# Local attention: the floor under the sums of squares as a maximum over pairs, its power of two moved into the logarithm and the Newton step

## The reference, cut to what matters

```python
def l2norm(t):
    return t / jnp.clip(jnp.linalg.norm(t, axis=-1, keepdims=True), 1e-12)

def _layer(x, wqkv, qs, ksc, wo, lg, lb, w1, b1, w2, b2):
    h = shift_token(x)
    q, k, v = jnp.split(h @ wqkv, 3, axis=-1)
    q, k, v = (to_heads(q), to_heads(k), to_heads(v))
    q = l2norm(q) * qs
    k = l2norm(k) * ksc
    q, k = rotary_xpos(q, k)
    o = local_attention(q, k, v)
    ...
```

## Time and profile before

| | |
|---|---|
| median of 3 runs (lowest, highest) | 3533.75 us (3529.92, 3533.93) |
| the profiled execution | 3536.04 us, span 3534.4 us, mean granted clock 0.947 |
| PE busy | 3087.3 us, 87% |
| DVE busy | 2690.6 us, 76% |
| ACT busy | 1625.1 us, 46% |
| POOL busy | 839.8 us, 24% |
| L2017 | 128 times, 168.5 us, mean 1316 ns |
| L2025 idle before it, waiting for L1827 | 54.9 us, 40 times |
| local attention, first layer | L2014 from 2057.97 to 2568.16 us |
| local attention, second layer | L2014 from 2775.85 to 3307.19 us |

### The profile page before, as it was taken

The page is one execution under the profiler, slowest core; times in us unless marked ns, Lnnn a source line. Parts: engine busy times, 40 slices in busy tenths (PEclk is TensorE's granted clock), DMA queues, the critical chain, the costliest instruction groups (busy, mean ns, idle before and its releaser), DMA issues. The chain is left out here.

```text
span 3534.4 us, 95348 instructions
## 1 busy us (share of the span) xinstructions
PE 3087.3 (87%) x34384; PEld 2089.7 (59%) x34384; DVE 2690.6 (76%) x5841; ACT 1625.1 (46%) x2545; POOL 839.8 (24%) x892
## 2 busy tenths in 40 slices
PE   4998769998999979999899668898979788888787
PEld 2666656665666656666566446666655456656545
DVE  5887767886777767766688779999956689989655
ACT  2665115664333335543466435555532355555422
POOL 1000000000000000001000156666611466666311
PEclk9999559998999989999899879999999999999999
DMA  4110001110000021110111100000001000000022
GB/s 137 30 29 20 0 5 31 29 29 4 0 0 0 0 44 38 41 22 1 28 27 29 62 13 7 9 9 8 4 19 27 13 11 10 9 11 8 19 65 59
DMA packets 193061, 80.16 MB, mean 23 GB/s; under 512 B 179124, under 2 KB 181864, under 8 KB 192232
## 3 DMA queue, kind: packets, MB, share of 16 engines
q1 hardware_dynamic: 191592, 73.25, 8.9%
q0 software_dynamic: 1280, 4.20, 0.3%
HBM read 35.58 MB, written 8.39 MB: 12 GB/s over the span
## 5 line engine op out<-in xcount | busy, mean ns | idle before, releaser
L770 ACT ACTIVATE probs_t<-ps_pt 128x1024 f32<-128x1024 f32 x256 | 262.2, 1024 | 384.8 <-PE ps_pt L884 384.8
L632 DVE TENSOR_REDUCE row_max<-ps_s 128x16 f32<-128x1024 f32 x256 | 313.2, 1224 | 135.2 <-PE ps_s L873 132.5
L1961 POOL TENSOR_TENSOR kblk<-kblk 128x1024 f32<-128x1024 f32 x128 | 301.6, 2356 | 199.1 <-DVE kblk L2002 199.1
L637 DVE TENSOR_TENSOR probs<-ps_s,row_max 128x1024 f32<-128x1024 f32 x256 | 312.1, 1219 | 11.7
L906 PE MATMUL ps_o<-v,probs_t 128*64 128x18 f32 x8192 | 285.4, 212 | 5.4 <-issue 5.2
L616 POOL TENSOR_TENSOR x<-x,out_bias_L 128x512 f32 (+1 forms) x32 | 40.7, 1272 | 1030.3 <-DVE x_norm L426 520.8
L906 PEld LDWEIGHTS ps_o<-v,probs_t 128*64 128x64 f32 x8192 | 260.1, 138 | 40.3 <-issue 19.0
L884 PE MATMUL ps_pt<-ident,probs 128*128 128x128 f32 x2048 | 277.1, 278 | 2.9 <-ACT probs L765 2.9
L873 PE MATMUL ps_s<-kblk,q_t 64*64 64x512 f32 x2048 | 273.5, 607 | 7.0 <-issue 6.9
L765 ACT ACTIVATE probs<-probs 128x1024 f32<-128x1024 f32 x256 | 269.6, 1053 | 16.6 <-DVE probs L637 15.1
L1979 POOL TENSOR_TENSOR kblk<-kblk,small_d 128x1024 f32<-128x1024 f32 x128 | 243.6, 1903 | 50.7 <-POOL small_d L1971 50.7
(11 more groups left out here) (307 smaller groups left out, 6930.7 us busy)
## 6 DMA issues: line engine op xcount, KB each, us to landing
ci<-in_ctx_t SPq DMA_DIRECT2D x64, 256.0 KB, 3.0
kblk<-k_t SPq DMA_DIRECT2D x768, 16.0 KB
ci<-x SPq DMA_DIRECT2D x64, 128.0 KB
ci<-x SPq DMA_DIRECT2D x128, 63.0 KB
x<-in_x_in SPq DMA_DIRECT2D x4, 1024.0 KB, 8.0
mask<-in_mask_l SPq DMA_DIRECT2D x64, 64.0 KB, 2.5
kblk<-ci SPq DMA_DIRECT2D x256, 16.0 KB
out<-x SPq DMA_DIRECT2D x1, 4096.0 KB, 11.1
```

Of the source, the lines that this page charges most:

```text
L632: dve.tensor_reduce(row_max[u % 2][:, :], scores_of(u), AX, ALU.max).then_inc(max_ready.sem, 1)
L637: dve.tensor_tensor(probs[u % 2][:, :, :], scores_of(u), row_max[u % 2][:, :].unsqueeze(2).broadcast_to([P, HEADS, S]), ALU.subtract).then ...
L770: act.activation(probs_t[:, :, :], ps_pt[:, :, :].rearrange("p a (r t) -> p (a r) t", t=P), ACT.Copy).then_inc(pt_ready.sem, 1)
L1961: pool.tensor_tensor(a, a, b_, ALU.add).then_inc(rotated.sem, 1)
```

## The change

The sums of squares are written to every second element of a new buffer `floored` (128 x 16 x 2), whose other elements hold the floor 1e-24, filled once in `prepare_layers`. A maximum over pairs (a reduction) replaces the two-operation instruction that took the maximum and multiplied by 2^20. The power of two goes into the scale of the logarithm's input and into the factor of the Newton step.

```diff
+        floored = sb("floored", [P, 2 * LHEADS, 2])
...
                 @block.vector
                 def _(dve):
+                    dve.memset(floored[:, :, 1], 1e-24).then_inc(tables.sem, 1)
...
-            nwork, nrm, nlog, nroot, nstep = (small[n][:, 0, :] for n in "abcde")
+            nrm, nlog, nroot, nstep = (small[n][:, 0, :] for n in "bcde")
...
-                        act.activation(nlog, nrm, ACT.Ln).then_inc(l_root.sem, 1)
+                        act.activation(nlog, nrm, ACT.Ln, scale=float(2 ** LOG_SCALE)).then_inc(l_root.sem, 1)
...
-                        step(pool.tensor_scalar(nstep, nstep, -0.5, 1.5, ALU.mult, ALU.add))
+                        step(pool.tensor_scalar(nstep, nstep, -0.5 * 2 ** LOG_SCALE, 1.5, ALU.mult, ALU.add))
...
                         wait_tile(dve, squared, g, t)
-                        dve.tensor_reduce(nwork, square, AX, ALU.add).then_inc(norms.sem, 1)
+                        dve.tensor_reduce(floored[:, :, 0], square, AX, ALU.add).then_inc(norms.sem, 1)
                         wait_tile(dve, norms, g, t, 1)
                         wait_tile(dve, l_newton, g, t - 1)
-                        dve.tensor_scalar(nrm, nwork, 1e-24, float(2 ** LOG_SCALE), ALU.max, ALU.mult)\
-                           .then_inc(norms.sem, 1)
+                        dve.tensor_reduce(nrm, floored[:, :, :], AX, ALU.max).then_inc(norms.sem, 1)
...
-                    dve.wait_ge(tables.sem, 6 * DEPTH)
+                    dve.wait_ge(tables.sem, 1 + 6 * DEPTH)
```

## The result

The changed kernel takes 3472.76 us (3470.89 to 3476.71) where the one before takes 3532.48 on the same chip; the ratio is 0.9833, 95% interval 0.9816 to 0.985. On a second chip it was 0.9841 (0.9828 to 0.9855). The profiled execution's span fell from 3534.4 to 3472.2 us, by 62.2. In the first layer the distance from the first sum of squares to the last fell from 510.2 to 481.0 us, in the second from 531.3 to 502.9: 57.6 together. Lines are two or three higher than before: L2014 is now L2017, L2017 is L2020, L1961 is L1964, L1967 is L1970, L1979 is L1982, L2042 is L2044, L1808 is L1811, L2025 is L2027, L1787 is L1790.

A forecast was written before the change was run, and what follows sets the result against it. VectorE was taken to set three tiles of four, TensorE the fourth. Afterwards TensorE's 29.71 us plus one 0.65 wait make 30.36 a foursome, saving 2.04 x 32 = 65 us, minus about 2: 3471 us, range 3440 to 3505.

The forecast's parts named there:

- L2017's wait goes: VectorE, local attention: the reduction runs beside GpSimd's L1961 and takes 0.19 us; VectorE gains 1.13 us a tile.
- TensorE next: TensorE's own work limits next: 7.03 us a tile, 1.59 more in the window's tile, 29.71 a foursome (four tiles).
- The collision: VectorE's product L2042 asks before GpSimd's L1967 and holds it; L1979 starts at +4.65 after L2014, L1808 waits 0.65 us.
- The root will come early: ScalarE's root L1906 reaches GpSimd at about +2.3 after L2014, so the 0.70 us wait of L1967 goes.
- One wait a foursome: TensorE's L1808 waits 0.65 us for GpSimd, counted once per four tiles: 29.71+0.65 = 30.36 us.
- VectorE waits for the scores: Sign of being right: VectorE's L2025 waits for TensorE's scores (L1827) in nearly every tile.
- The standstills of the second layer: TensorE stands still six times for no shown wait; VectorE's bound will hide less of each: minus about 2 us.
- Ends of the pipelines: Time between the layers and behind the second; the prediction gave it no term.
- The slower rival: VectorE's L2042 loses repeatedly to GpSimd's instructions, 1.5 us late, 8.2 us a tile, 48 us more: 3582; chance 5%.

The follow-up runs named there:

- reordered kernel: The kernel before, with VectorE's sum of squares and floor (L2014, L2017) put ahead of the rotation (L2002): 3577.91 us, ratio 1.0128.

## Why the prediction was right, point by point

The time of 3471 us was met within 2 us, and its mechanism held: the wait of L2017 goes, and TensorE with one wait for GpSimd sets what is left. Its steps held as follows.

- *L2017's wait goes.* Right: 0.19 us for the new line as worked out, L2040 at +1.43 (forecast +1.44) and L2044 at +2.38 (+2.38). That the reduction starts freely under a running GpSimd instruction had no row before; L2020 under L1964 is one. The price of the old wait, 1.13 us a tile, is confirmed by the run with the sums first.
- *TensorE next.* Right: 7.02 us a tile (7.03), and 8.70 in the window's tile, a detour of 1.68 (1.59). TensorE's own foursome is 29.76 (29.71), as the doubled transposes show.
- *The collision.* Right in order and size in the tile that counts: L2044 asks first, takes 0.79 us, and L1970 takes 0.67; L1982 at +4.59 (+4.65). L1811 waits 0.54 (0.65). Without the collision 0.45 us a foursome go. "The root will come early" holds in three tiles of four. In the fourth, L1970 waits 0.70 us for ScalarE's L1909 as before, takes 0.22, and L1982 starts at +4.90. This costs nothing, as TensorE is late there from the window's detour and waits for nothing.
- *One wait a foursome.* Mis-sized. The forecast was 30.36; foursomes are 30.45 and 30.79 in turn, 30.62 on average, 8 us more over 32. After the tile of 7.62 comes one of 7.11 or 7.46, not of 7.03. The 7.11 has no wait that the trace names; in the 7.46, L1811 waits 0.38 us a second time. That wait comes from a term that the sum didn't have. In GpSimd's timeline, once in eight tiles:

```profile
2467.52 0.22 POOL L1974 TENSOR_TENSOR small_d<-small_d,small_e 128x16 f32<-128x16 f32 x1
2468.52 1.90 POOL L1982 TENSOR_TENSOR kblk<-kblk,small_d 128x1024 f32<-128x1024 f32 x1 [0.78 <-POOL small_d L1974]
```

  The gap before L1982 is 0.78 us instead of 0.35, and L1982 starts at +5.03 where four tiles later it is +4.69. Eight tiles are two windows, the length of the body of the engines' loop. The same gap stood in the trace before (L1979 5.76 us after L2014, where four tiles later it is 5.43) and cost nothing there: foursomes were 32.4 us either way. As TensorE waits for this path now, the gap shows.
- *VectorE waits for the scores.* Forecast for nearly every tile; it is three of four (92 of 128).
- *The standstills of the second layer.* Taken as a loss of 2 us; the second layer gained 0.8 us less than the first.
- *Ends of the pipelines.* Left at nothing; 4.6 us of the 62.2 lie outside the two distances, 3.8 of them between the last sum of squares of a layer and its last residual (20.2 and 20.3 us before, 18.35 twice after). Not all of that is the change's: the run with only the power of two moved, which kept the old instruction, has 19.1 twice. These ends and the point before made up for most of the 8 us of the foursomes. That the total is within 2 us is luck to that extent; the foursome, 1.78 us saved of 2.04 forecast, is the fair measure.
- *The slower rival.* It didn't come: L2044 gets in at the end of L1964, where it asked 0.24 us before, and doesn't lose to the short instructions behind it. No run shows that it can lose to them. The reordered kernel shows a loss of the same size, at 1.0128, from one long instruction. The rival's price was also worked out wrongly: 0.4 x 128 is 51, not 48, and a longer tile of VectorE's costs only in three tiles of four, as the reordered kernel has it (8.25, 8.25, 8.25, 8.86), so 0.37 x 96 = 36 us and 3570 us would have followed from its own premises.

## What to carry to other kernels

An instruction whose time is far above that of its size may be waiting inside its duration: compare its end with the ends of what runs on GpSimd, and try another form of the same arithmetic, or cut GpSimd's instruction in two. Then ask where the instruction behind it lands; moved 1.1 us earlier, the product with two operands in SBUF met the last quarter of a microsecond of GpSimd's addition here, and the program was 1.7% faster. With another order it met all but the first 0.7 us of it, and the program was 1.3% slower although the same wait was gone. And bound the gain by the next engine's own sum for a whole period, for an engine freed by 1.13 us a tile gave 0.45.

## What the runs showed of the hardware that was not expected

- Of two GpSimd instructions that stand back to back, a VectorE instruction that has been waiting gets in after the first: it asks 0.21 us before the first half's end and takes 0.23 us, within a pair that takes 2.50 together.
- A product of two operands in SBUF that asked during GpSimd's L1961 ended 0.56 us after it (2.22 us, of 0.69 alone), so 0.13 us of its length passed before the other's end. After the change it was the same: 0.55 behind L1964's end at 2504.52.
- Four transposes repeated in place cost TensorE 0.44 us, where their start and the next instruction's are 0.58 apart.
- With four of a tile's instructions doubled, TensorE stood still for 3.7 to 3.8 us once or twice in the middle of the first layer, which has no such standstill without them. Those of the second layer, 1.9 to 3.0 us, are in every trace of these kernels, always at the turn of the loop.
